# Transposes of two late groups of rows one tile later, and three idle products in the drain in place of thirty

## The reference, cut to what matters

```python
def _act_quant(x):
    scale = 127.0 / jnp.clip(jnp.max(jnp.abs(x), axis=-1, keepdims=True), 1e-05)
    xq = jnp.clip(jnp.round(x * scale), -128.0, 127.0) / scale
...
def _L0_ffn_ref(x, w_gate, w_up, w_down):      # inner size 1024
    gate = jax.nn.silu(_bitlinear(x, w_gate))  # both operands quantized
    up = _bitlinear(x, w_up)
    return _bitlinear(gate * up, w_down)
...
x = x + jnp.tanh(g_xattn[0]) * _L0_xattn_ref(_layernorm(x), ctx_1024, ctx_1024, ...)
x = x + jnp.tanh(g_ffn[0]) * _L0_ffn_ref(_layernorm(x), w_gate, w_up, w_down)
```

## Time and profile before

| | us |
|---|---|
| median of 3 runs | 817.08 |
| the runs | 817.41, 812.32, 817.08 |
| profiled execution, its own time | 817.38 |
| its span, first to last instruction | 815.6 |

### The profile page before, as it was taken

The page is one execution under the profiler, slowest core; times in us unless marked ns, Lnnn a source line. Parts: engine busy times, 40 slices in busy tenths (PEclk is TensorE's granted clock), DMA queues, the critical chain, the costliest instruction groups (busy, mean ns, idle before and its releaser), DMA issues.

```text
span 815.6 us, 21012 instructions
## 1 busy us (share of the span) xinstructions
PE 719.1 (88%) x7154; PEld 478.7 (59%) x7154; DVE 718.2 (88%) x1479; ACT 692.4 (85%) x1482; POOL 522.4 (64%) x983
## 2 busy tenths in 40 slices
PE   7458899999999999999999999999998887886897
PEld 5234566666666666666666666666665555443454
DVE  4779899989989899989999999899998868698895
ACT  1468899898999999999999998989898987577793
POOL 3747656667776767666767676766752245476794
PEclk9665799999999999999999999999999999799899
DMA  9997947465757575776555665746461123166565
GB/s 194 188 255 161 196 131 146 108 122 129 151 120 142 124 145 124 138 134 127 138 132 127 127 133 120 147 121 145 120 125 29 46 78 108 46 147 150 133 163 151
DMA packets 148889, 108.52 MB, mean 133 GB/s; under 512 B 56991, under 2 KB 145183, under 8 KB 148767
## 3 DMA queue, kind: packets, MB, share of 16 engines
q1 hardware_dynamic: 143630, 101.98, 57.0%
q10 hardware_dynamic: 5152, 5.19, 2.7%
HBM read 49.54 MB, written 12.85 MB: 76 GB/s over the span
## 4 chain that ended last, share of the span: by engine, by line
PE 34%; ACT 33%; DVE 16%; issue 9%; POOL 3%; DMA 2%; SPq 1%; ACTq 0%; DVEq 0%; POOLq 0%
ACT ex L1178 13%; ACT pt L1168 11%; PE p_o L1326 6%; PE p_m L1404 5%; PE p_s L1309 5%; DVE kst L1014 3%; PE p_t L1347 3%; PE p_m L1385 3%; DVE hmax L1017 3%; PE p_m L1393 3%; ACT L1205 2%; DVE stats L889 2%; ACT L1168 2%; PE p_m L1377 2%; DVE nm L908 2%
## 5 line engine op out<-in xcount | busy, mean ns | idle before, releaser
L1178 ACT ACTIVATE ex<-p_s,nm 112x375 f32<-112x375 f32 x512 | 273.4, 608 | 12.6 <-DVE nm L908 10.9
L1168 ACT ACTIVATE pt<-p_t,ct 128x336 f32<-128x336 f32 x488 | 243.2, 565 | 31.6 <-PE p_t L1347 31.2
L889 DVE BATCH_NORM_STATS2 stats<-ex 112x6 f32<-112x375 f32 x512 | 252.7, 535 | 8.1 <-ACT ex L1178 6.6
L908 DVE TENSOR_REDUCE nm<-p_s 112x2 f32<-112x750 f32 x256 | 235.9, 922 | 1.3 <-PE p_s L1309 1.3
L1309 PE MATMUL p_s<-kst,qst 96*112 96x375 bf16 x512 | 135.2, 348 | 35.4 <-ACT ex L1178 24.4
L1347 PE MATMUL p_t<-qst,kst 99*128 99x112 bf16 x1464 | 114.7, 213 | 4.6 <-ACT pt L1168 3.8
L1347 PEld LDWEIGHTS p_t<-qst,kst 99*128 99x128 bf16 x1464 | 90.5, 97 | 43.4 <-issue 18.4
L1385 PE MATMUL p_m<-wv_sb,ctxt 128*128 128x256 f32 (+1 forms) x384 | 107.9, 405 | 3.6 <-DVE va L841 2.2
L1326 PE MATMUL p_o<-pt,va 128*32 128x112 f32 (+1 forms) x3072 | 101.6, 265 | 1.0 <-ACT ex L1178 0.5
L1404 PE MATMUL p_m<-ctxt,wk_sb 128*128 128x375 f32 x240 | 93.7, 514 | 1.2 <-DVE qf L857 0.7
L1326 PEld LDWEIGHTS p_o<-pt,va 128*32 128x32 f32 (+1 forms) x3072 | 70.3, 110 | 36.3 <-issue 30.2
(11 more groups left out here) (190 smaller groups left out, 1217.1 us busy)
## 6 DMA issues: line engine op xcount, KB each, us to landing
kst<-kp SPq DMA_DIRECT2D x378, 93.8 KB, 3.5
ctxt<-ctxt_dram SPq DMA_DIRECT2D x32, 375.0 KB, 4.3
qbounce<-qp SPq DMA_DIRECT2D x32, 168.0 KB, 2.6
qst<-qbounce SPq DMA_DIRECT2D x32, 168.0 KB, 3.6
qst<-qbounce SPq DMA_DIRECT2D x32, 112.0 KB, 3.4
xm<-x_dram SPq DMA_DIRECT2D x32, 112.0 KB, 2.5
x_dram<-x SPq DMA_DIRECT2D x32, 112.0 KB, 1.9
xt<-x_dram SPq DMA_DIRECT2D x28, 128.0 KB, 3.0
```

The lines of the kernel that those rows point to most:

```text
L889: last = nc.vector.bn_stats(stats[:, nb % RING, 2 * pb + i], ex[0:SQ, 2 * (t % 2) + i, :])
L908: nc.vector.tensor_reduce(nm[:, n % RING, 2 * p:2 * p + 2], p_s[t % 2][0:SQ, :, 0:SK], axis=AX.X, op=ALU.max, negate=True).then_inc(s_max, 1)
L1168: nc.scalar.activation(pt[:, (2 * r + i) % 8], st_home(r, i)[:, 0:KC * SQ].rearrange("k (c q) -> k c q", c=KC), ACT.Exp, scale=ct[:, nr % ...
L1178: last = nc.scalar.activation(ex[0:SQ, 2 * ((t - 1) % 2) + i, :], p_s[(t - 1) % 2][0:SQ, i, 0:SK], ACT.Exp, bias=nm[:, ne % RING, h:h + 1])
```

## The change

Two edits. The transposes of a late group are queued by TensorE four steps behind the group's start in place of three, and the copies by VectorE five in place of four: for group 12 at the end of step 14 and the beginning of step 15, for group 13 at the end of step 17 and the beginning of step 18. In the drain, a table gives the count of idle products: two behind the down product of step 28 and one behind that of step 31, none elsewhere.

```diff
--- before.py
+++ after.py
@@ -352,6 +352,7 @@
         BETWEEN = {SLOTS * (B + 3) + 4: 0, SLOTS * (B + 3) + 6: 1, SLOTS * (B + 3) + 7: 2, SLOTS * (B + 4) + 1: 3, SLOTS * (B + 4) + 2: 4, SLOTS * (B + 4) + 5: 5, SLOTS * (B + 5) + 4: 6, SLOTS * (B + 6) + 4: 7}
         X_AT, SQ_AT = TAIL, 9
         VAR_AT, SQRT_AT, RSTD_AT, RSTD_LATE = SLOTS * B + 6, SLOTS * B + 7, SLOTS * (B + 3) + 2, 18
+        IDLE = {TILES: 2, TILES + 3: 1}
         LATE_AT = {10: TAILED, 13: TAILED + 1}
 
         def stat_slot(b):
@@ -1002,8 +1003,8 @@
                     rows_var(EARLY_TILES, TILES, 1)
                 if s == RSTD_LATE:
                     rows_scale(EARLY_TILES, TILES, 1)
-                if s - 4 in LATE_AT:
-                    copy_group(LATE_AT[s - 4])
+                if s - 5 in LATE_AT:
+                    copy_group(LATE_AT[s - 5])
                 n = s
                 if 0 <= n < TILES:
                     dve.wait_ge(s_sg, count(1, n, 1))
@@ -1501,15 +1502,15 @@
                     for k in range(FC):
                         last = nc.tensor.matmul(p_y[n % 2][:, 0:D], hqt[n % HRING][:, k * P:(k + 1) * P], wq8[2][:, k * D:(k + 1) * D], start=(k == 0), stop=(k == FC - 1))
                     last.then_inc(s_y, 1)
-                if TILES - 1 < s < TILES + Y_LAG:
+                if s in IDLE:
                     if s == TILES:
                         pe.wait_ge(s_h, TILES)
-                    for _ in range(6):
+                    for _ in range(IDLE[s]):
                         nc.tensor.matmul(p_u[:, 0, :], identb[:, :], wq8[0][:, 0:512], start=True, stop=True)
-                if s - 3 in LATE_AT:
-                    if LATE_AT[s - 3] == TAILED:
+                if s - 4 in LATE_AT:
+                    if LATE_AT[s - 4] == TAILED:
                         pe.wait_ge(s_otc, B)
-                    transpose_group(LATE_AT[s - 3])
+                    transpose_group(LATE_AT[s - 4])
 
             timeline(slot, tile)
```

## The result

The changed kernel takes 810.33 us (median of 17 runs) where the kernel before takes 815.61 us on the same chips: a ratio of 0.9932, with a 95% interval of 0.9917 to 0.9947. That is 5.5 us less by the ratio (5.3 us between the two medians), 0.7%. The forecast was 810.8 us and within 1%.

What follows compares the result with a forecast made beforehand. The prediction took VectorE, at 2.93 us per tile, to bound the steady stretch. From 817.38 us it took 3.1 for the groups and 3.5 for the drain, giving 810.8 us, range 805.5 to 815.5.

Steps and rivals of the forecast that it cites:

- The sum: Whole kernel: 817.38 us less 3.1 for the groups and 3.5 for the drain gives 810.8 us, 0.8% less.
- The steady stretch and what lies outside it: VectorE fills the steady tiles at 2.93 us each; only its idle time outside them, and the drain, can be won.
- Group 12: Transposes one tile later start at 754.51 us without a wait; tile 14's gated product comes 1.5 us earlier.
- Group 13: Transposes one tile later do not wait; tile 17 leads by 3.7 us; both groups together win 3.1 us.
- The clock among the groups: TensorE stays at full clock despite a new 1.9 us idle stretch ahead of tile 15's up product.
- The drain: After the last tiles: fewer idle products let the last down product start 3.8 us earlier, bound by transposed rows; gain 3.5 us.
- rival (c): TensorE runs at 1.2 GHz in the whole drain and behind both new gaps: 818.8 us, chance 0.07.
- Rival (a): Clock falls ahead of tile 15's up product or the last store lands late: 812.8 or 812.9, both 814.9 us; chance 0.18.
- Rival (b): Late groups' transposes still wait for GpSimd's rows, so only the drain is won: 813.9 us, chance 0.07.
- bunched stores: End of the drain: 0.3 us taken off the gain because stores issued close together can land late.
- rival (d): Whole kernel: the median falls on a level 5 us lower seen in one run, 805.8 us; chance 0.20.

Runs made afterwards that it cites:

- both repairs: Changed kernel with late row scales made by scalar_tensor_tensor with a PSUM input, plus thirteen idle products queued before the drain's first down product: ratio 0.9925.
- fillers: Thirteen idle products queued ahead of the drain's first down product: ratio 0.9939 on the changed kernel, 0.9983 and 0.9989 with the groups edit alone, 1.0005 on the kernel before.
- repaired scales: Changed kernel with late row scales made by scalar_tensor_tensor with one PSUM input: ratio 0.9921; the same without any idle products: 0.9909.

## Why the prediction was right, and where its terms were off

**The sum.** The closeness of 810.8 to 810.33 us is in part luck. The forecast took 6.6 us from 817.38, an execution 1.8 us above the later median of the kernel before; the measured gain is 5.5 us. Of the two terms the group's was too large by about 1.1 us in every trace of the changed groups with the old row scales; the drain's was 0.6 too large in the changed kernel's profile and 0.4 too small where the clock stayed up.

**The steady stretch and what lies outside it.** Right: 26.4 us from tile 18 to 27 in every trace, whatever else was changed.

**Group 12.** Right in its steps, with one size off. The transposes start 3.09 us behind the gated product of 13 without a wait, and tile 14 comes 1.43 us earlier in relation to tile 13 (1.5 forecast). Tile 15 then gives back only 0.20 us for the moved copy where 0.5 was forecast, in part because 0.12 us of waiting ahead of it went too. The experiment with the copies alone shows that the gain is the transposes' place in TensorE's queue. How much of it is the wait itself and how much the low clock behind it no run separates: the two come and go together in all fourteen traces.

**Group 13.** The step that failed is the sentence "I take it whole, because from tile 18 on the stage is the steady one that VectorE fills", with "VectorE's own work is the same". The 3.7 us forecast as tile 17's lead were there (1.43 - 0.20 + 0.01 + 2.58 = 3.8 us from the four distances). Then VectorE's work was not the same: the two row scales took 1.88 us in place of 0.45, and 1.88 to 1.90 in all seven traces that have the new groups and the old form, but 0.45 or 0.46 in the four with the groups as before. I had called 3.1 us the upper bound from VectorE's idle time and looked for a lower one only in the clock. The idle time of VectorE ahead of tile 17 was also GpSimd's idle time ahead of tile 18, and it was that which had made the row scales cheap. With the form that does not meet GpSimd the stretch takes 21.25 us: 3.4 us won, 0.3 more than forecast. So 3.1 us was no upper bound either: VectorE's rows from tile 12 to 18 add up to 20.92 us before and with the repair, and the time between them falls from 3.74 to 0.33 us, of which I had counted only the two long waits.

**The clock among the groups.** Right. The new idle stretch was 2.06 us (1.9 forecast) and the clock stayed at 1.00 in all ten traces that have it. Where the transposes stood in their old step (four traces) the low stretches came back each time.

**The drain.** The mechanism was right and is shown by the drain edit alone: 4.78 us between first and last down product, the last waiting for its rows, 3.9 us won against 3.5. In the changed kernel's own profile the term was 2.9, since the clock fell there: the step "by the rows nothing falls, and the sum stays 810.8" took the full clock of the drain before for granted. It was rival (c)'s mechanism for the drain. It cost 1.0 us and not the 4.3 that rival (c) gave it (from 3.8 us earlier to 0.5 later): the clock was back by the third down product. Rival (a)'s late landing did not befall the last store (1.7 us in the changed kernel too); in one trace, with both repairs, it befell the transposed rows. Rival (b) was wrong in every trace with the transposes in their new step. The 0.3 us taken off for bunched stores was not seen. Of rival (d) there are single executions (down to 806.74 us) and no median.

**What the change made worse.** The groups edit brings the tiles to the drain 2.0 us sooner, and all four profiles with exactly that lead and no fillers (the changed kernel, the groups alone twice, and the kernel without idle products) have the low clock there, while two traces with no lead (before, the drain edit alone) and the two with a lead of 3.4 us (repaired scales, no fillers) don't. The kernel with the copies alone, 0.4 us late, has it too, a little further in. So the lead sorts these traces. The time from the span's start does not: tile 27's gated product started at 795.91 us in a trace where the clock fell and at 795.71 in one where it stayed. That a lead of 2.0 us is merely one unlucky moment of arrival is my reading and was not tested by moving the arrival alone, nor is it shown why it repeats so well for one kernel. The trace shows an idle stretch of 3.28 us ahead of the first down product in all of them; it is the same stretch at another moment. The Trainium skill, "TensorE: Matmul & The Clock Gate", section "Why this matters for your kernels", tells to avoid idle gaps between bursts of matmuls. The runs agree in that with 0.48 us in place of the gap the clock did not fall in any of five traces, but they also show the same gap of 3.28 us without a fall in four.

## What to carry to other kernels

In a queue worked in order, look at what stands behind a wait: here four transposes of 0.4 us held two products and with them two other engines, and one step of delay removed the wait. When a stall goes, ask which cheap instruction was cheap because another engine idled with it; the price appears in the next stretch and not where the edit is. And compare stretches between two rows of the same trace when executions differ by more than the edit is worth: the groups edit could be read to 0.1 us so, where 12 runs left 1.5 us open. For a stretch that differs from one execution to the next, as the drain does here by its clock and its landing, one trace shows what can happen and not how often.

## What the runs showed of the hardware

**VectorE waits for GpSimd in some forms of instruction.** A tensor_scalar on 128 x 6 values, SBUF to SBUF, takes 0.22 or 0.23 us while GpSimd is idle, and 1.10 or 0.78 us beside a busy GpSimd: it ends 0.02 to 0.03 us behind GpSimd's instruction. The tensor_tensor on 128 x 6 values just ahead of it (L951 before, L952 after), both inputs in SBUF, does the same in every trace: it took 0.38 us in the kernel before, ending at 772.81 where GpSimd's L733 ended at 772.79, and 0.30 us in the kernel before with fillers, again ending 0.02 us behind GpSimd's L733. No trace here has it beside an idle GpSimd. The same scales through scalar_tensor_tensor with one input from PSUM take 0.22 us beside a GpSimd that works without a break. The Trainium skill, "SBUF — State Buffer", section "Who interferes with whom", says that VectorE and GpSimd share a pair of SBUF ports which one of them holds for a whole instruction, and that tensor_scalar can be among the forms that take it. The trace agrees, down to two values per partition (L981 of the changed kernel, 0.35 us, ends at 752.03 where GpSimd's L727 ended at 752.01); the one-value tensor_scalar (L1020, 0.15 us) did not wait in any trace.

**The clock comes back by itself in a thin drain.** With no idle product at all, five down products brought TensorE back within three of them: the granted clock was 0.51 from 799.8 to 803.2 us and 1.00 from 803.8 us on.
